# A linear-attention and mixture-of-experts layer: one-hot row tables in place of token and gate in the scattered rows, k and v in pairs of tiles, expert weights converted partly inside the loop

## The reference

```
xn = layernorm(x)                                  # no scale, no shift
# attention without softmax, in 2 batches of 1024 tokens, 16 heads of 16
q = k = elu(xn @ Wqk + bqk);  v = silu(xn @ Wv + bv);  u = silu(xn @ Wu + bu)
kv = sum over tokens of k^T v   (16x16 per head and batch)
attn = (u * layernorm(q @ kv, ln_g, ln_b)) @ Wo + bo
# 8 experts, 2 per token
probs = softmax(xn @ gate_w^T);  w, e = top_k(probs, 2);  w = w / sum(w)
ffn = sum over the 2 chosen e of  w * ((silu(xn @ w1[e]^T) * (xn @ w3[e]^T)) @ w2[e]^T)
out = x + attn + ffn
```

## Time and profile before

| | |
|---|---|
| median of 3 runs | 314.05 us (310.64 to 314.34) |
| profiled execution, its time | 312.15 us |
| its span in the profile | 310.1 us |
| TensorE busy | 239.5 us (77%) |
| VectorE busy | 181.7 us (59%) |
| ScalarE busy | 156.4 us (50%) |
| GpSimd busy | 149.1 us (48%) |

### The profile page before, as it was taken

How to read it: one execution, slowest core, us unless ns; L and a number is a source line. 1 busy time by engine, 2 the same in 40 slices (tenths; PEclk the granted TensorE clock), 3 DMA queues, 4 the chain that set the end, 5 groups by cost and what they waited for, 6 DMA issues and landing times.

```text
span 310.1 us, 5880 instructions
## 1 busy us (share of the span) xinstructions
PE 239.5 (77%) x1656; PEld 148.0 (48%) x1656; DVE 181.7 (59%) x433; ACT 156.4 (50%) x288; POOL 149.1 (48%) x128
## 2 busy tenths in 40 slices
PE   0328999497950029999999999999999999899730
PEld 0118457155640004566766656657665455455420
DVE  3898999939990004867768585867674333323200
ACT  2876956994890003546364645454464344343300
POOL 6374458888987710062432244425450465045561
PEclk9999799879995559999999999999999999999955
DMA  6999941569842235595887978799999899969763
GB/s 200 412 423 427 426 199 61 145 136 306 236 105 104 102 84 112 99 145 80 141 100 112 149 117 130 120 136 128 114 133 125 137 121 145 158 119 142 103 68 34
DMA packets 90001, 49.11 MB, mean 158 GB/s; under 512 B 78098, under 2 KB 87314, under 8 KB 88788
## 3 DMA queue, kind: packets, MB, share of 16 engines
q1 hardware_dynamic: 80020, 33.36, 49.7%
q0 software_dynamic: 9952, 15.38, 28.9%
HBM read 18.01 MB, written 15.38 MB: 108 GB/s over the span
## 4 chain that ended last, share of the span: by engine, by line
PE 50%; POOL 18%; DMA 12%; DVE 9%; issue 7%; POOLq 2%; SPq 0%; ACT 0%; DVEq 0%
PE bank L1114 31%; POOL slots L411 17%; PE bank L1127 13%; DMA regions<-slots 8%; PE bank L1165 3%; DMA area<-x 3%; DVE kT L689 2%; PE bank L1142 2%; POOLq L432 1%; PE bank L1154 1%; DVE area L812 1%; DMA slots<-xrow,slot 1%; DVE wa L695 1%; DVE stats L677 1%; DVE xT L704 1%
## 5 line engine op out<-in xcount | busy, mean ns | idle before, releaser
L1114 PE MATMUL bank<-regions 128*128 x468 | 108.8, 383 | 26.6 <-DMA regions<-slots 24.5
L441 POOL DMA_INDIRECT out<-xrow x39 | 62.3, 1597 | 111.4 <-issue 59.1
L1114 PEld LDWEIGHTS bank<-regions 128*128 128x128 f16 x468 | 44.3, 99 | 77.7 <-issue 31.9
L917 DVE SCALAR_TENSOR_TENSOR regions<-bank,regions 128x512 f32<-128x512 f32 x39 | 27.0, 692 | 63.9 <-PE bank L1114 63.4
L1127 PE MATMUL bank<-regions 128*128 x468 | 58.7, 276 | 4.1 <-DMA regions<-regions 4.1
L1127 PEld LDWEIGHTS bank<-regions 128*128 128x128 f16 x468 | 45.8, 99 | 17.4 <-issue 5.8
L596 ACT ACTIVATE regions<-regions 128x512 f16<-128x512 f32 x39 | 24.6, 630 | 56.8 <-DVE regions L917 54.9
L591 ACT ACTIVATE regions<-bank 128x512 f32<-128x512 f32 x39 | 23.3, 597 | 51.4 <-PE bank L1114 51.1
L411 POOL DMA_INDIRECT slots<-xrow,slot x32 | 42.3, 1322 | 12.8 <-issue 9.4
L922 DVE TENSOR_TENSOR regions<-regions 128x512 f16<-128x512 f32 x39 | 26.9, 690 | 22.0 <-ACT regions L596 22.0
L1035 PE MATMUL bank<-wa,xT 128*128 128x512 f16 x96 | 26.3, 415 | 0.0
(11 more groups left out here) (142 smaller groups left out, 292.6 us busy)
## 6 DMA issues: line engine op xcount, KB each, us to landing
regions<-wexp SPq DMA_DIRECT2D x8, 1536.0 KB, 20.9
out<-xT POOLq DMA_DIRECT2D x8, 256.0 KB, 6.9
area<-x SPq DMA_DIRECT2D x2, 768.0 KB, 8.0
regions<-wattn SPq DMA_DIRECT2D x1, 1032.0 KB, 11.1
out<-padrow POOLq DMA_DIRECT2D x1, 896.0 KB
regions<-slots SPq DMA_TRANSPOSE x39, 3.7
regions<-regions SPq DMA_TRANSPOSE x39
xrow<-slots SPq DMA_DIRECT2D x39, 1.0 KB, 2.5
```

Source lines behind the costliest of these rows:

```text
L441: g.indirect_dma_start(out, bass.IndirectOffsetOnAxis(ap=meta[:, t, 0:1].bitcast(I32), axis=0), ysb[t % RING], None, compute_op=ALU.add).t ...
L917: v.scalar_tensor_tensor(h32[t % 2], ps_b[t % 2][:], 1.0 / SCALE, s32[t % 2], ALU.mult, ALU.mult).then_inc(h_ready, 1)
L1114: last = mm(bank_[:], xg[t % 4][:, KD * d + k, :], w16[:, bass.ds(e, 1), w, at:at + I].rearrange("p a c -> p (a c)"), start=(k == 0 and n ...
```

## The change

Rows go out without token and gate: `xrow16` holds the two halves alone, 1 KB a row, and 32 scatters fill the table, 16 and 16, with the copy of x between them. Since padding is no longer scattered, SP writes zeros to the whole table first, between the loads of expert 0 and expert 1. Token and gate weight of each slot come from a product: a slot number is split in its tile and its place; `hi_hot` (32 x 39) and `lo_hot` (32 x 128) are one-hot tables, `rows16` is `hi_hot` times the token number and times the weight's two halves, and `invert` multiplies the two in 32 matmuls into one bank, from which `row_tables` makes the index and the weight of every slot. Padding goes to 256 spare rows of the output. k and v are computed in pairs of tiles, k in one bank and v in another; all of u goes before the second pair. L406 goes; GpSimd does no arithmetic after the x stage. Four experts are converted before the loop and four in its steps 0 to 3, `hidden` waits for one expert more at each of the first eight tiles, and the attention pairs start at step 4. The gate weights, the tables and the loop's buffers have new places.

```
-PAIR_AT = [2 + 3 * p for p in range(NP)]
+EARLY = 4
+PAIR_AT = [4 + 3 * p for p in range(NP)]
...
# SP
+            load_expert(0)
+            sp.wait_ge(zeros_set, 1)
+            sp.dma_start(xslots.rearrange("(s p) c -> p s c", p=P), zeros.unsqueeze(1).broadcast_to([P, ST, 2 * D])
+                         ).then_inc(slots_cleared, 16)
+            for e in range(1, E - 2):
                 load_expert(e)
             sp.wait_ge(attn_lo, 1 + KD)
-            load_expert(E - 1)
+            sp.wait_ge(rows_done, 1)
+            for e in range(E - 2, E):
+                load_expert(e)
...
+            for c in range(TT // CH):
+                transpose_k(c)
             for t in range(3):
                 load_x(t)
-            transpose_k(3)
             for t in range(ST):
                 turn_h(t)
                 if t + 3 < ST:
                     load_x(t + 3)
-                load_meta(t)
...
# GpSimd
-            pool.wait_ge(w_scaled, 1)
-            g.tensor_tensor(w16[:, 0, 1, 0:POOL_COLS], ...).then_inc(w_lo_pool, 1)
...
             pool.wait_ge(slot_ready, 1)
+            pool.wait_ge(slots_cleared, 16)
             for t in range(TT):
-                scatter(slot[:, 0, t:t + 1], xrow[:, t, :]).then_inc(scattered1[t // CH], 16)
+                scatter(0, t)
             g.dma_start(out[0:TOKENS, :] ...)
-            for c in range(PADS):
-                scatter(padslot[:, c:c + 1], padrow[:, 2 * c:2 * c + ROW]).then_inc(pads_scattered, 16)
-            for c in range(TT // CH):
-                pool.wait_ge(gate2_placed, c + 1)
-                for t in range(CH * c, CH * (c + 1)):
-                    scatter(slot[:, 1, t:t + 1], xrow[:, t, :]).then_inc(scattered2, 16)
+            g.dma_start(out[TOKENS:TOKENS + SPARE, :], x[0:SPARE, :]).then_inc(y_added[1], 16)
+            for t in range(TT):
+                scatter(1, t)
...
# ScalarE, before the loop
+            exps(0)
+            act.wait_ge(slots_cleared, 16)
+            hi(1)
+            for p in range(4): u_out(p)
+            halves(0)
+            for p in range(4, NP): u_out(p)
+            exps(1); hi(2); exps(2); halves(1); exps(3); halves(2)   # halves(2) waits for the tables
+            hi(3); exps(4); halves(3); exps(5); halves(4); kv_halves(0)
+            exps(6); halves(5); exps(7); halves(6); halves(7); (silu table); kv_halves(1)
# and in the loop
+                if t < E - EARLY:
+                    act.wait_ge(w_lo, EARLY - 1 + t)
+                    hi(EARLY + t)
...
# VectorE
+            v.tensor_tensor(hi_hot, per_row(slot_hi[:]), tile128[...], ALU.is_equal).then_inc(hi_hot_ready, 1)
+            v.tensor_tensor(lo_hot, slot_lo[...].broadcast_to([P, TOPK * TT, P]), col_no[...], ALU.is_equal)
+            for n, value in enumerate((token1[:], gates16[:, 0, :], gates16[:, 1, :])):
+                v.tensor_tensor(rows16[:, :, n, :], hi_hot, per_row(value), ALU.mult).then_inc(rows_ready, 1)
+            expert_lo(0); maps(1); row_tables(); k_lo(0); expert_tables(); maps(2); expert_lo(1); k_lo(1)
+            maps(3); k_lo(2); expert_lo(2); maps(4); k_lo(3); kv_blocks(0); maps(5); k_lo(4); kv_lo(0)
+            maps(6); k_lo(5); expert_lo(3); maps(7); k_lo(6); k_lo(7); kv_blocks(1); kv_lo(1)
# and at the end of each loop step
+                if t < E - EARLY:
+                    expert_lo(EARLY + t)
...
# TensorE
+            def project_pair(p, bank_, bias, col, done):
+                wait(pe, kv32_ready, 2 * (p - 1))
+                mm(bank_[:], ones[0:2, :], bias.unsqueeze(1).broadcast_to([2, 2, D]), start=True, stop=False)
+                for j in range(2):
+                    for k in range(KD):
+                        for n, (w, d) in enumerate(PASSES):
+                            last = mm(bank_[:, j * D:(j + 1) * D], xT[:, 2 * p + j, KD * d + k, :],
+                                      wa16[:, w, k * AC + col:k * AC + col + D], ...)
+            def invert():
+                pe.wait_ge(rows_ready, 1 + NV)
+                for n in range(TOPK * TT):
+                    last = mm(ps_rows[:, 0:NV * ST], lo_hot[:, n, :], rows16[:, n, :, :]..., ...)
+                last.then_inc(rows_done, 1)
+            for p in range(NP):
+                u_proj(p)
+            pe.wait_ge(uT_ready, 2 * NP)
+            kv_proj(1)
+            for p in range(NP):
+                if p + 2 < NP:
+                    kv_proj(p + 2)
+                if p == 0:
+                    invert()
+                kv(p)
...
             def hidden(t):
+                if t < E:
+                    pe.wait_ge(w_lo, t + 1)
```

More of the change, by code:

```diff
@@ L230, in build @@
         kl_ready = sem("kl_ready")
-        kT_done = sem("kT_done")
+        kT_done = [sem(f"kT_done{i}") for i in range(2)]
         kv_mm = sem("kv_mm")
@@ L410, in scatter @@
-            def scatter(index, row):
-                return g.indirect_dma_start(slots, bass.IndirectOffsetOnAxis(ap=index, axis=0), row, None)
-            pool.wait_ge(slot_ready, 1)
+            g.tensor_tensor(qv_bias16[:], qv_bias, qv_bias32, ALU.subtract).then_inc(bias_lo, 1)
+            def scatter(k, t):
+                g.indirect_dma_start(xslots, bass.IndirectOffsetOnAxis(ap=slot[:, k * TT + t:k * TT + t + 1], axis=0),
+                                     xrow16[:, t, :], None).then_inc(scattered, 16)
@@ L768, in _ @@
             first, second, i1, i2, gap, ge1 = [tmp([TT]) for _ in range(6)]
-            slotf = tmp([TOPK, TT])
+            slotf = tmp([TOPK * TT])
             over = tmp([E, TT])
-            tiles, base, end, lower, freed = [tmp([E]) for _ in range(5)]
+            tiles, base, end = [tmp([E]) for _ in range(3)]
             sums = tmp([E, E])
@@ L830, in _ @@
                 [P, TOPK, TT * E]), ALU.mult))
-            chain(v.tensor_reduce(slotf.rearrange("p k t -> p (k t)"),
-                                  part.rearrange("p k (t e) -> p (k t) e", e=E), AX.X, ALU.add))
+            chain(v.tensor_reduce(slotf, part.rearrange("p k (t e) -> p (k t) e", e=E), AX.X, ALU.add))
             v.tensor_copy(slot[:], slotf).then_inc(slot_ready, 1)
-            chain(v.tensor_tensor(sums, before[:], total.unsqueeze(1).broadcast_to([P, E, E]), ALU.mult), k_map, 0)
@@ new lines, in _, with per_row @@
+            dve.wait_ge(slot_ready, 1)
+            chain(v.tensor_scalar(lo_int[:], slot[:], P - 1, None, ALU.bitwise_and), v_map, 0)
+            chain(v.tensor_copy(slot_lo[:], lo_int[:]))
+            chain(v.scalar_tensor_tensor(slot_hi[:], slot_lo[:], -1.0, slotf, ALU.mult, ALU.add))
+            def per_row(u):
+                return u.unsqueeze(2).broadcast_to([P, TOPK * TT, ST])
+            v.tensor_tensor(hi_hot, per_row(slot_hi[:]), tile128[:].unsqueeze(1).broadcast_to([P, TOPK * TT, ST]),
+                            ALU.is_equal).then_inc(hi_hot_ready, 1)
@@ L928, in center @@
                 if p == 0:
[L929 removed]
+                    for i in range(2):
+                        dve.wait_ge(kT_done[i], 8 * (TT // CH))
                 for j in range(2):
```

487 lines of the change are left out of this document (230 added, 257 removed).

## The result

The kernel after takes 324.21 us, the median of 4 runs (320.51 to 326.65); the kernel before took 313.19 beside it. The ratio, of the fast runs of both alone, is 1.036, 95% interval 1.028 to 1.043: slower. The forecast was 308, and its range ended at 317. The profiled execution took 320.51 us with a span of 318.7.

A forecast was written before the change was run, and what follows sets the result against it. Bound by a front part, GpSimd's queue of 39 scatters, a TensorE-bound loop and a tail. Loop start -13.4, loop +8.4 and tail +1.0 give -4.0: 312.15 to 308.2 us; forecast's own range 303 to 313, overall 299 to 317.

The forecast's parts named there:

- The loop start: Start of the expert loop: 101 us where 114.43 was, 13.4 us sooner, range 97 to 108.
- the tail: End of the kernel: GpSimd's adds lag the copies of rows by 1 us more (0 to 3).
- routing: Before the first scatter: dropping L406 cuts L812 from 3.08 to 0.2 us; gain 1.9 us, bounds 1.0 to 2.8.
- the queue of scatters: GpSimd before the loop: 32 scatters with their waits sum to 55.5 us, the last landing at 97.
- Rival (b): Before the scatters: clearing the slots comes late, at 140 GB/s ending at 52, for a time of 321; chance 0.12.
- the end of the k and v part: Before the loop: last lower half of k at 94, then 2 us allowed for transpose and tile load; loop starts 101.
- Rival (c): Before the loop: the k and v part is the new bound, a loop start at 107 gives 314; chance 0.18.
- Rival (a): First loop tiles: the extra passes are mostly absorbed, only 0 to 2 us lost, giving 301 to 302; chance 0.20.
- the loop's first tiles: Loop steps 0 to 3: converting experts 4 to 7 there puts tile 6 at start + 32.9; loop 8.4 us longer.
- The 2.0 us of attention work: Loop behind tile 6: 2.0 us more attention work than before, part of the loop's 8.4 us.

## Why the prediction was wrong, step by step

Set against its own sum of 308.2, the profiled 320.5 is 12.3 us more. The loop start accounts for +15.5 (116.49 for 101), tile 6 behind it for +0.7 (33.6 for 32.9), the rest of the loop for -1.8, the tail for -1.7 and the time outside the span for -0.2 (with the roundings of the sum, 12.3).

**Partly right, in part by luck: routing and the queue of scatters.** The timeline:

```profile
35.34 0.17 DVE L806 TENSOR_SCALAR area<-gate 128x16 f32<-128x16 f32 x1
...
40.12 0.18 DVE L828 CAST slot<-area 128x32 int32<-128x32 f32 x1
...
41.35 1.23 POOL L420 DMA_INDIRECT xslots<-xrow,slot  x1 [14.10 <-issue]
...
41.93 1.46 DVE L837 TENSOR_TENSOR xg_all<-slot_hi,tile 128x1248 f16<-128x1248 f16 x1
...
43.31 4.42 DVE L839 TENSOR_TENSOR regions<-slot_lo,col_no 128x4096 f16<-128x4096 f16 x1
...
44.54 4.02 POOL L420 DMA_INDIRECT xslots<-xrow,slot  x1 [0.30 <-issue]
```

The gate operation fell from 3.08 to 0.17 us. The first scatter started at 41.35 and not at 39.6, hardly earlier than the 41.46 of the earlier trace rows. VectorE waited 1.27 us for TensorE's ranks, which came 1.2 us later than before, behind the longer first pair of k and v, so the slot numbers ended at 40.30 and not at 39.3. The scatter then began 1.05 us behind them, where it had been 0.3 before; what it waited for the trace does not show. The gain was 0.9 us for the slot numbers and 0.1 for the scatter (forecast 1.9, bounds 1.0 to 2.8, a miss). The tables cost 1.46 and 4.42 us, as worked out (1.46, 4.4); the Trainium skill's twofold rate (VectorE: DVE Perf Modes, perf-mode tier table) did not come, and the page's condition for it (What auto-detection actually checks), that every tensor steps by one, is not met by the broadcast input here. The stretched scatter beside the table shows the wait as in the earlier trace rows. The last scatter started at 93.61, forecast about 94. That is two errors that cancel: the queue began 1.8 us late and took 53.2 us from first to last, where the prediction had 55.5 (its terms add up to 56.0).

**Rival (b), the clearing, was dead.** Its row among the issues:

```profile
xslots<-regions SPq DMA_DIRECT2D x1, 4992.0 KB, 25.3
```

Issued at 7.1 us, it is in at 32.4, about 200 GB/s beside the loads, between the two ends that the prediction had worked out (29 and 37.8); nobody waited.

**The step that failed is the end of the k and v part**: "SP's last transpose of k goes then, and the tile load behind it; I allow 2 us (bounds 0 and the 5.6 us ...)". I gave the landing of a transpose no place except at the end, though `halves(4)` and `halves(6)` each wait until an earlier transpose has read the buffer, and I took the transposes of before, 4 to 6 us, as their price anywhere. In the kernel before, they hardly met the copy (the second, issued at 64.6, landed at 71.07, 0.6 us behind the copy's issue; the third was issued at 81.41, when the copy was in). The change puts both behind the same point, near 69 us, with the expert loads that I had myself placed "near 60 us, at some 4 us each" and given 40 us of cover: I asked whether the loads would come late, not what they would meet. The second of them was in flight until 71.3, past the issue of both the transpose and the copy. What the runs showed in its place is one landing of 28.6 us that ScalarE waits 19.2 us for in the middle of the part, and a loop start at 116.49. Without the copy the loop starts at 99.16, and at 100.55 and 101.20 in the two profiled executions with rows of 1 KB, for a forecast of 101. But there the scatters bring the start, for which the prediction had 100; the k part, given as the later of the two at 101, is the earlier one there. That the number for the start comes out so well is in part luck.

**Rival (c)** said that a handover of this part might be longer, at 107 for the loop's start. The place was right, the size (116.5) was not in it, and the mechanism, a collision of transfers, stood in no rival. Rival (a) was wrong:

**Right: the loop's first tiles.** The timeline of the pass for expert 4 (the one for expert 7 stands in the chain above, at 139.60), of the first centering and of the turn:

```profile
123.83 3.35 DVE L726 SCALAR_TENSOR_TENSOR regions<-regions 128x3072 f16<-128x3072 f32 x1
...
142.87 0.76 DVE L931 BATCH_NORM_STATS2 area<-bank 128x6 f32<-128x256 f32 x2
...
149.09 0.99 PE L1161 MATMUL bank<-ident,area 128*128 128x128 f16 x8 [3.93 <-DVE area L947]
```

VectorE's passes end at 10.7, 16.0, 21.2 and 26.5 behind the start (forecast 9.8, 15.3, 20.7, 26.2), the centering follows at 26.4, and TensorE idles 3.9 us before the turn (forecast 4.6). Tile 6 at 33.6 (forecast 32.9) was 32.3 to 33.6 in the seven other runs of after with four early experts and pairs from step 4. The 2.0 us of attention work that I added behind tile 6 did not appear: tile 6 to the last copy of rows took 158.0 us, before 157.8.

**The tail.** Expected 1 us more lag; it was 0.5 less:

```profile
308.06 0.47 ACT L603 ACTIVATE regions<-bank,row_gate 128x256 f32<-128x256 f32 x1 [4.45 <-PE bank L1133]
...
311.37 1.55 POOL L445 DMA_INDIRECT out<-regions,row_out  x1 [0.60 <-DMA out<-regions,row_out]
```

3.3 us from copy to add where the earlier trace rows had 3.8.

With the stall out, the forecast of 308.2 was 2 to 5 us too high (303 to 306 in four profiled executions without the stall, the copy in its place or left out): the terms up to tile 6 hold, and the 2.0 us behind it and the longer tail did not come. The sign of the result was decided by a term that was not in the sum.

## What to carry to other kernels

When an edit moves transfers, list for each what else is in flight at its new time on all queues, and who waits for its landing and not only for its end in the queue; a landing time read from an idle stretch is no price for a crowded one. Ask of every part that comes level with the longest one what slack it used to have: the same collision cost the kernel before nothing. And give a DMA effect several executions before believing a cure; one execution of the copy in rows of 1 KB gave nearly the forecast's loop start and tile 6, and proved nothing.

## What the runs showed of the hardware

- A DMA transpose of k (4.3 to 7.3 us where no copy of x was near) took 28.6 us beside a DRAM to DRAM copy of 2.1 MB, the end of two expert loads and the scatters; the copy took 19.3 instead of 9.2 us, while the DMA engines showed shares of 0.98 to 1.45 at 35 to 53 GB/s. Beside the copy and the scatters alone a transpose took 13.1 to 15.6 us, among the expert loads and the scatters alone 10.1 and 11.4.
- With the copy in rows of 1 KB and six early experts the same program had two groups of times, 10 to 12 us apart (near 300 and near 312), 5 and 3 executions, in mixed order.
- A comparison of 16-bit values with an input that is broadcast along its last dimension took 4.42 us for 4096 elements and 1.46 for 1248, 1.04 ns for each further element.
